# A graph network's convolutions and node sums: weighted sums and totals on ScalarE and VectorE in place of TensorE

## The chip, the core and the metric

One core of a Trainium2 chip runs the whole program. The core has five engines that work from queues of their own: PE (TensorE, matmuls), DVE (VectorE), ACT (ScalarE), POOL (GpSimd) and SP (SyncE, which here only issues DMAs). They meet through semaphores. The metric is device time in microseconds (us) of one execution, lower is better; the time before is the median of three.

## What is computed

The input is a graph: 50,000 nodes with 128 features (`x`) and 25,000 edges sorted by their destination. Two parts follow each other: a sorting convolution with two layers, and a gated recurrent part with five steps. Only the first part is touched by the change:

```
h = relu(layernorm(x))
for layer in 0, 1:
    # up to 4 messages of each node, missing ones filled with blank_p, sorted per feature
    srt = sort(filled, axis=1)                       # (node, 4, 128)
    out = einsum('nmd,m->nd', srt, cw) + cb          # weighted sum of the 4 sorted rows
    u = a * h + out
    mu, var = mean and variance of u over all 50000 nodes, per feature
    h = h + (u - mu) / sqrt(var + 1e-5) * g + be
x = x + h
# then: x + GRU(relu(layernorm(x))), 5 message passing steps
```

All of it is in 32-bit floats.

## The kernel before, in words

The program runs in stages. Stage 1 makes the layer-normed rows `h0_tab` and counts the edges. Then comes one block for each layer: `convolve`, `statistics`, and `apply0` or `apply1`. The recurrent part (all lines from 1400 on) follows.

**`convolve`** handles the edges as 28 groups (NC) of 128 partitions times 7 edges (JC), 896 numbers in each partition. POOL gathers the source rows (L721, seven indirect DMAs a group, into a ring `M` of four) and later scatters the results into `o_tab` (L729, seven more, from a ring `ob` of three, OR). Its program is gather(0), gather(1), gather(2), then gather(i), scatter(i-3) in turn. DVE sorts a group with eleven instructions (L818 to L845) and leaves the four sorted rows in `V[i % 2][0..3]`; the table operands stand in PSUM (`S1`, `L2`, `H2`), so each of these instructions reads at most one operand from SBUF. ACT fills the PSUM operands with the blank row (L750, L776, L777), copies the row before a group (`halo`, L762), and, in `rows(i)` (L784), turns the finished PSUM sum into `ob`. PE forms that sum: eight matmuls per group (L860), each a sorted row times a diagonal matrix `cwi[m]` of the weight. Each f32 matmul stands as two records in the trace. ACT runs `rows(i-1)` after it has prepared group i. SP meanwhile writes the blank rows of the next layer's table.

**`statistics`** reads all rows back in 49 chunks (NCH) of 128 x 1024 numbers: SP loads `hb` and `ob` (512 KB each, rings of four, SR), DVE forms u in `ob` (L907), ACT squares it into `sq` (L938), PE adds u and its square over partitions into two PSUM banks (L948, four matmuls a chunk, a matrix of ones; for the last chunk `ones_last`, which leaves the padding out). SP loads the next chunk when PE has read the old one (`s_pe`). In the same time POOL issues single-column indirect DMAs whose number is fixed: in layer 0 it gathers 196 columns (L661) in all, 120 of them in `statistics` and 76 in `apply0`; in layer 1 it scatters 70 (L658).

**`apply0`** normalises in 49 chunks; DVE has four instructions a chunk (L2233, L2235, L2237, L1050). Before chunk 16 (NCH // 3) DVE runs `slots()`, which waits for all 196 gathered columns; POOL then waits for `slots()` and scatters 126 columns (L658). `apply1` does the same for layer 1 with row statistics, PE transposes and messages (L1174, L1181, L1184) and eight indirect DMAs a chunk on POOL (L1254).

The order on each engine is the order of the code. There is no scheduler.

## Time and profile before

| what | us |
|---|---|
| median of three runs | 5515.18 (5511.57 to 5521.06) |
| span of the one profiled execution | 6564.5 |
| stage 1 | 0 to 337 |
| layer 0: convolve, statistics, apply0 | 337 to 911, to 1292, to 1546 |
| layer 1: convolve, statistics, apply1 | 1546 to 2133, to 2368, to 3121 |
| recurrent part | 3121 to 6564 |

The profile has one execution, taken with the recorder on. Nothing gives this execution's time apart from its span of 6564.5 us. That span is 1049 us longer than the median of the runs without a recorder, so a row of the trace tells of an execution that is a fifth slower than those that are measured. Where the two differ has to be argued, and is, below. Busy shares over the whole span are PE 65%, DVE 59%, ACT 42%, POOL 51%; no engine bounds all stages.

### The profile page before, as it was taken

Reading aid. Unit: us, or ns where it says so; the run is one execution under the profiler, and the core shown is the slowest. Engines: PE = TensorE matmul, PEld = TensorE weight load, DVE = VectorE, ACT = ScalarE, POOL = GpSimd, SP = SyncE. Lnnn points to the kernel's source line nnn. Section 1 sums busy time; section 2 is a strip of 40 time slices with the busy share of each in tenths; the row PEclk is TensorE's granted clock in tenths of the full one; section 3 lists DMA queues with packets and bytes.
Section 4 is the critical chain, followed back from the end, with each engine's and each line's share of the span. In section 5 each row is a group of like instructions: output and inputs, shape, how many; then the busy total and the mean of one; then the engine's idle time right before and its main releaser. Section 6 shows DMA issues by size and latency. Waiting matters only on the chain. (4 is left out here: it accounts for less than half of the span.)

```text
span 6564.5 us, 61506 instructions
## 1 busy us (share of the span) xinstructions
PE 4257.9 (65%) x15022; PEld 2341.7 (36%) x15022; DVE 3845.9 (59%) x7518; ACT 2733.4 (42%) x5325; POOL 3376.4 (51%) x3399
## 2 busy tenths in 40 slices
PE   8944352602344754343577899789889978884586
PEld 5612121300121333232344455455445544442333
DVE  8965530397564255564466676667667756652265
ACT  6822210222222134343476654664465456433432
POOL 8766677046666434544665600640262056556666
PEclk9966676855666877677799999999999999997699
DMA  6722231694111585654476654664465456664444
GB/s 217 256 97 88 80 117 46 238 307 153 40 41 38 195 246 164 179 170 132 140 205 192 213 183 138 201 199 166 150 217 193 138 187 202 214 189 135 123 144 145
DMA packets 628093, 1062.87 MB, mean 162 GB/s; under 512 B 105048, under 2 KB 258158, under 8 KB 627740
## 3 DMA queue, kind: packets, MB, share of 16 engines
q1 hardware_dynamic: 498972, 818.46, 38.6%
q0 software_dynamic: 100544, 163.41, 9.0%
q10 hardware_dynamic: 28224, 77.08, 3.0%
q8 instruction: 126, 2.06, 0.1%
q14 instruction: 227, 1.86, 0.1%
HBM read 599.34 MB, written 464.81 MB: 162 GB/s over the span
## 5 line engine op out<-in xcount | busy, mean ns | idle before, releaser
L1864 POOL DMA_INDIRECT r_G<-msg_tab,srow x784 | 739.6, 943 | 1324.9 <-DMA msg_tab<-r_m 895.0
L860 PE MATMUL l_ps<-cv_V,cv_cwi 128*128 128x448 f32 x896 | 478.3, 702 | 916.7 <-ACT cv_ob L784 457.4
L1254 POOL DMA_INDIRECT x_tab<-a_r,node_pos x392 | 379.6, 968 | 514.7 <-DVE a_r L1211 246.7
L860 PEld LDWEIGHTS l_ps<-cv_V,cv_cwi 128*128 128x128 f32 x896 | 220.4, 253 | 1174.7 <-issue 1161.6
L2113 DVE TENSOR_TENSOR agg<-r_psS,agg 128x128 f32 x980 | 281.7, 287 | 514.7 <-DMA st_o<-o_tab 324.7
L729 POOL DMA_INDIRECT o_tab<-cv_ob,put_idx x392 | 387.7, 989 | 271.9 <-ACT cv_ob L784 147.8
L1945 PE MATMUL r_psR<-r_hin,whh 128*128 128x512 f32 x882 | 463.5, 608 | 27.3 <-ACT r_r L2066 11.4
L1896 PEld LDWEIGHTS r_psM<-wmsg,r_hnew 128*128 128x128 f32 x2744 | 355.8, 195 | 339.5 <-DVE r_hnew L2177 219.1
L1896 PE MATMUL r_psM<-wmsg,r_hnew 128*128 128x128 f32 x2744 | 384.0, 284 | 133.4 <-DVE r_hnew L2177 126.2
L721 POOL DMA_INDIRECT cv_M<-h_tab,gat_src x392 | 373.9, 954 | 119.5 <-issue 119.5
L1181 PE MATMUL l_ps<-a_bmsg,row 128*128 128x512 f32 x196 | 152.5, 871 | 429.3 <-ACT cv_M L1137 271.6
L907 DVE SCALAR_TENSOR_TENSOR st_o<-st_h,ab,st_o 128x1024 f32<-128x1024 f32 x98 | 125.9, 1285 | 507.9 <-DMA st_o<-o_tab 453.2
L784 ACT ACTIVATE cv_ob<-l_ps,cbb 128x896 f32<-128x896 f32 x56 | 56.4, 1007 | 817.5 <-remote 670.4
L948 PE MATMUL l_ps<-st_q,ones 128*128 128x512 f32 x384 | 213.0, 683 | 211.4 <-issue 181.1
L1917 PE MATMUL r_psR<-r_oin,whh 128*128 128x512 f32 x290 | 189.4, 740 | 245.5 <-issue 156.0
L658 POOL DMA_INDIRECT sort_tab<-pair,sort_at x196 | 195.6, 998 | 277.6 <-DVEq L1040 214.1
L1945 PE MATMUL r_psZ<-r_hin,whh 128*128 128x512 f32 x642 | 330.4, 596 | 11.9 <-issue 3.9
L818 DVE COPY_PREDICATED l_ps<-l_ps,cv_M 128x896 f32<-128x896 int32 x56 | 61.5, 1099 | 452.3 <-ACT cv_M L762 399.7
L2129 DVE TENSOR_TENSOR r_m<-r_psM,bmsg 128x512 f32<-128x512 f32 x343 | 235.7, 687 | 150.7 <-remote 80.3
L938 ACT ACTIVATE st_q<-st_o 128x1024 f32<-128x1024 f32 x98 | 103.3, 1056 | 514.5 <-remote 168.6
L1971 PE MATMUL r_psS<-r_sel,r_G 128*128 128x128 f32 x1960 | 293.0, 298 | 28.2 <-DMA r_G<-msg_tab,srow 17.7
L2051 ACT ACTIVATE r_dist<-iota_w,lrank 128x128 f32<-128x128 f32 x980 | 310.0, 390 | 0.0
(292 smaller groups left out, 11307.7 us busy)
## 6 DMA issues: line engine op xcount, KB each, us to landing
r_hin<-ht_tab SPq DMA_DIRECT2D x441, 256.0 KB
msg_tab<-r_m SPq DMA_DIRECT2D x392, 256.0 KB
ht_tab<-r_hnew SPq DMA_DIRECT2D x343, 256.0 KB
o_tab<-o_blank SPq DMA_DIRECT2D x98, 512.0 KB, 6.0
st_h<-h_tab SPq DMA_DIRECT2D x98, 512.0 KB
st_o<-o_tab SPq DMA_DIRECT2D x98, 512.0 KB
r_oin<-ht_tab SPq DMA_DIRECT2D x161, 256.0 KB
i_x<-x_tab SPq DMA_DIRECT2D x49, 528.0 KB
```

What stands on the lines that cost most here:

```text
L721: pool.indirect_dma_start(M[i % CR][:, 1 + q, :], None, h_tab[layer], bass.IndirectOffsetOnAxis(ap=gat_src[:, j:j + 1], axis=0)).then_inc( ...
L729: pool.indirect_dma_start(o_tab[layer], bass.IndirectOffsetOnAxis(ap=put_idx[:, j:j + 1], axis=0), ob[i % OR][:, q, :], None, bounds_check ...
L860: ins = nc.tensor.matmul(psO[:, h, 0:HW], cwi[m][:], V[i % 2][m][:, HW * h:HW * (h + 1)], start=m == 0, stop=m == 3)
L948: ins = nc.tensor.matmul(ps, w[:], t[:, 512 * q:512 * (q + 1)], start=i == 0 and q == 0, stop=i == NCH - 1 and q == 1, skip_group_check=True)
L1254: pool.indirect_dma_start(x2_tab, bass.IndirectOffsetOnAxis(ap=node_pos[:, j:j + 1], axis=0), rb[i % RR][:, t, :], None).then_inc(s_out[i ...
L1864: pool.indirect_dma_start(G[g % GR][:, q, :], None, msg_tab[s % 3] if s else first_tab, bass.IndirectOffsetOnAxis(ap=at, axis=0)).then_inc ...
L1896: ins = nc.tensor.matmul(psM[:, t, :], hnew[k % 2][:, P * t:P * (t + 1)], wmsg[:], start=True, stop=True)
L1945: ins = nc.tensor.matmul(ps, whh[:, g * D:(g + 1) * D], hin[k % 3][:], start=True, stop=not edges)
L1971: nc.tensor.matmul(psS[g % 2][:, q, :], G[g % GR][:, q, :], sel[g % 2][:, q, :], start=True, stop=True).then_inc(s_sel, 1)
L2051: nc.scalar.activation(dist[:, q, :], iota_w[:, 0:SW], ACT.Abs, bias=lrank[:, TQ * i + q:TQ * i + q + 1]).then_inc(s_di, 1)
L2113: nc.vector.tensor_tensor(agg[:, bass.ds(at[q], SW)], psS[g % 2][:, q, :], agg[:, bass.ds(at[q], SW)], ALU.add).then_inc(s_ev, 1)
L2129: nc.vector.tensor_tensor(mb[k % 2][:], psM[:], other, ALU.add).then_inc(s_me, 1)
```

## The change

In `convolve` PE has no work left. ACT multiplies the smallest sorted row by its weight, adds `cb` and writes `ob` (`smallest`, in place of `rows`), and it does so at the end of its turn i, not i+1. DVE adds the other three rows with three dependent `scalar_tensor_tensor` instructions that read `V` and `ob`, both in SBUF. The wait for the ring `ob` (scatter i-3 landed) stands before `smallest`. In `statistics` DVE adds each chunk's u and squares into two running sums of 128 x 1024 in SBUF (they lie in two free `M` buffers), and PE adds these over the partitions once, at the end, with four matmuls. SP reloads `hb` after u is formed and `ob` after u has been added and squared. The four diagonal matrices and `ones_last` go.

```diff
@@ convolve, scalar @@
-                def rows(i):
-                    act.wait_ge(s_mix, i + 1)
+                def smallest(i):
+                    act.wait_ge(s_v0, i + 1)
                     if i >= OR:
                         act.wait_ge(s_sc[i % OR], 16 * JC * (i // OR))
-                    nc.scalar.activation(ob[i % OR][:].rearrange("p j f -> p (j f)").rearrange("p (h n) -> p h n", n=HW),
-                                         psO[:, :, 0:HW], ACT.Identity, bias=cbb[layer][:, 0:1]).then_inc(s_o, 1)
+                    nc.scalar.activation(ob[i % OR][:].rearrange("p j f -> p (j f)"), V[i % 2][0][:], ACT.Identity,
+                                         bias=cbb[layer][:, 0:1], scale=cwb[layer][:, 0:1]).then_inc(s_o0, 1)
...
                     blank_second(i)
-                    if i:
-                        rows(i - 1)
-                rows(NC - 1)
+                    smallest(i)
@@ convolve, vector @@
                     if i >= 2:
-                        dve.wait_ge(s_mix, i - 1)
+                        dve.wait_ge(s_o0, i - 1)
...
                     dve.sem_inc(s_srt, 1)
+                    dve.wait_ge(s_o0, i + 1)
+                    o = ob[i % OR][:]
+                    for k in (3, 1):
+                        st.mark(nc.vector.scalar_tensor_tensor(o, v[k], cwb[layer][:, k:k + 1], o, ALU.mult, ALU.add))
+                        st.wait()
+                    nc.vector.scalar_tensor_tensor(o, v[2], cwb[layer][:, 2:3], o, ALU.mult, ALU.add).then_inc(s_o, 1)
@@ convolve, tensor @@
-                    for h in range(2):
-                        for m in range(4):
-                            ins = nc.tensor.matmul(psO[:, h, 0:HW], cwi[m][:], V[i % 2][m][:, HW * h:HW * (h + 1)],
-                                                   start=m == 0, stop=m == 3)
-                    ins.then_inc(s_mix, 1)
@@ statistics, sync @@
                     if i >= SR:
-                        sp.wait_ge(s_pe, i - SR + 1)
+                        sp.wait_ge(s_u, i - SR + 1)
                         sp.dma_start(hb[i % SR][:], hv[i]).then_inc(s_in[i % SR], 16)
+                        sp.wait_ge(s_au, i - SR + 1)
+                        sp.wait_ge(s_q, i - SR + 1)
@@ statistics, vector @@
+                def squares(i):
+                    m = LASTP if i == NCH - 1 else P
+                    dve.wait_ge(s_q, i + 1)
+                    if i:
+                        dve.wait_ge(s_aq, i)
+                    nc.vector.tensor_tensor(sums[1][0:m, :], sums[1][0:m, :], sq[i % 2][0:m, :], ALU.add).then_inc(s_aq, 1)
...
+                    if i:
+                        squares(i - 1)
+                    dve.wait_ge(s_u, i + 1)
+                    if i:
+                        dve.wait_ge(s_au, i)
+                    nc.vector.tensor_tensor(sums[0][0:m, :], sums[0][0:m, :], ob[k][0:m, :], ALU.add).then_inc(s_au, 1)
+                squares(NCH - 1)
@@ statistics, tensor @@
-                for i in range(NCH):
-                    w = ones_last if i == NCH - 1 else ones
-                    for t, s, ps in ((ob[i % SR], s_u, psU), (sq[i % 2], s_q, psQ)):
-                        pe.wait_ge(s, i + 1)
+                for t, s, ps in ((sums[0], s_au, psU), (sums[1], s_aq, psQ)):
+                    pe.wait_ge(s, NCH)
+                    for q in range(2):
+                        ins = nc.tensor.matmul(ps, ones[:], t[:, 512 * q:512 * (q + 1)], start=q == 0, stop=q == 1,
```

On ACT, in the middle of layer 0's convolution, a turn before reads as follows (`cv0_mixed` is PE's signal, `cv0_put0` a landed scatter):

```order
L776 ACTIVATE l_ps<-blank_p 128x896 [waits cv0_sorted]
L777 ACTIVATE l_ps<-blank_p 128x896
L778 ACTIVATE l_ps<-same 128x7
L784 ACTIVATE cv_ob<-l_ps,cbb 128x896 [waits cv0_put0,cv0_mixed]
L750 ACTIVATE l_ps<-blank_p 128x896 [waits cv0_pairs_done]
```

After the change, on the same engine at the same place (`cv0_smallest` is DVE's signal that the first sorted row is ready):

```order
L770 ACTIVATE l_ps<-blank_p 128x896 [waits cv0_sorted]
L771 ACTIVATE l_ps<-blank_p 128x896
L772 ACTIVATE l_ps<-same 128x7
L778 ACTIVATE cv_ob<-cv_V,cbb,cwb 128x896 [waits cv0_put0,cv0_smallest]
L744 ACTIVATE l_ps<-blank_p 128x896 [waits cv0_pairs_done]
```

The instruction that waits for the landed scatter is now that of the group just prepared, one group earlier than before.

On DVE, a group of the convolution before ends in two sorts and the next begins:

```order
L844 TENSOR_TENSOR cv_V<-cv_A,l_ps 128x896 [waits cv0_dve]
L845 TENSOR_TENSOR cv_V<-cv_A,l_ps 128x896
L818 COPY_PREDICATED l_ps<-l_ps,cv_M 128x896 [waits cv0_dve,cv0_halo,cv0_landed1,cv0_blank1]
```

After the change three instructions stand between them, the first of which waits for ACT (`cv0_rows_begun`):

```order
L832 TENSOR_TENSOR cv_V<-cv_A,l_ps 128x896 [waits cv0_dve]
L833 TENSOR_TENSOR cv_V<-cv_A,l_ps 128x896
L839 SCALAR_TENSOR_TENSOR cv_ob<-cv_V,cwb,cv_ob 128x896 [waits cv0_dve,cv0_rows_begun]
L839 SCALAR_TENSOR_TENSOR cv_ob<-cv_V,cwb,cv_ob 128x896 [waits cv0_dve]
L841 SCALAR_TENSOR_TENSOR cv_ob<-cv_V,cwb,cv_ob 128x896 [waits cv0_dve]
L805 COPY_PREDICATED l_ps<-l_ps,cv_M 128x896 [waits cv0_halo,cv0_landed1,cv0_blank1]
```

In the statistics DVE had one instruction a chunk (L907, 49 times in a row). Now it has three (the sums are called `cv_M`, after the buffers they lie in):

```order
L905 SCALAR_TENSOR_TENSOR st_o<-st_h,ab,st_o 128x1024 [waits st0_in2]
L897 TENSOR_TENSOR cv_M<-cv_M,st_q 128x1024 [waits st0_q_added,st0_q]
L912 TENSOR_TENSOR cv_M<-cv_M,st_o 128x1024 [waits st0_u_added,st0_u]
L905 SCALAR_TENSOR_TENSOR st_o<-st_h,ab,st_o 128x1024 [waits st0_in3]
```

The squares of a chunk are added behind the next chunk's u.

## Rows read from the trace of the kernel before

**Rows 1.** Head of the profile: the span.

```profile
span 6564.5 us, 61506 instructions
```

**Rows 2.** Window, length; PE, PEld, DVE, ACT, POOL busy (count); PEclk; DMA share; GB/s.

```profile
337.00:911.00 574.00, 239.59 (x450) 109.90 (x448) 331.08 (x337) 126.67 (x250) 381.13 (x393) 0.67 0.27 89
911.00:1292.00 381.00, 199.78 (x392) 84.14 (x392) 65.38 (x55) 51.88 (x50) 192.73 (x196) 0.75 0.41 139
1546.00:2133.00 587.00, 239.36 (x448) 110.48 (x448) 319.89 (x315) 127.47 (x252) 384.10 (x396) 0.66 0.15 43
2133.00:2368.00 235.00, 185.45 (x392) 79.71 (x392) 66.23 (x56) 52.04 (x50) 71.13 (x70) 0.87 0.65 220
2368.00:3121.00 753.00, 304.75 (x1335) 214.74 (x1335) 439.91 (x1234) 306.88 (x673) 380.57 (x393) 0.69 0.57 168
3121.00:6564.00 3443.00, 2787.43 (x10330) 1539.32 (x10330) 2084.39 (x3882) 1768.72 (x3361) 1569.61 (x1619) 0.93 0.55 175
```

**Rows 3.** Convolution, layer 0, in time: start, us, engine, line; idle before and its releaser.

```profile
623.71 1.10 DVE L818 COPY_PREDICATED l_ps<-l_ps,cv_M 128x896 f32<-128x896 int32 x1 [22.35 <-ACT cv_M L762]
...
632.31 0.99 POOL L721 DMA_INDIRECT cv_M<-h_tab,gat_src  x1 [0.30 <-issue]
...
635.41 1.10 DVE L818 COPY_PREDICATED l_ps<-l_ps,cv_M 128x896 f32<-128x896 int32 x1 [0.24 <-issue]
...
649.31 8.53 PE L860 MATMUL l_ps<-cv_V,cv_cwi 128*128 128x448 f32 x16 [5.30 <-ACT cv_ob L784]
650.18 0.99 POOL L721 DMA_INDIRECT cv_M<-h_tab,gat_src  x1 [0.31 <-issue]
...
675.63 0.94 POOL L721 DMA_INDIRECT cv_M<-h_tab,gat_src  x1 [0.30 <-issue]
682.65 1.01 ACT L784 ACTIVATE cv_ob<-l_ps,cbb 128x896 f32<-128x896 f32 x1 [30.00 <-remote]
...
684.46 1.01 POOL L729 DMA_INDIRECT o_tab<-cv_ob,put_idx  x1 [7.88 <-ACT cv_ob L784]
```

**Rows 4.** Statistics, layer 0, in time: with POOL issuing, then without.

```profile
1052.02 1.28 DVE L907 SCALAR_TENSOR_TENSOR st_o<-st_h,ab,st_o 128x1024 f32<-128x1024 f32 x1 [20.93 <-DMA st_o<-o_tab]
1052.18 1.94 POOL L661 DMA_INDIRECT look<-node_tab,src_at  x1 [0.30 <-issue]
1074.39 1.29 DVE L907 SCALAR_TENSOR_TENSOR st_o<-st_h,ab,st_o 128x1024 f32<-128x1024 f32 x1 [21.08 <-DMA st_o<-o_tab]
...
1220.61 1.06 ACT L938 ACTIVATE st_q<-st_o 128x1024 f32<-128x1024 f32 x1 [2.38 <-PE l_ps L948]
...
1224.05 1.06 ACT L938 ACTIVATE st_q<-st_o 128x1024 f32<-128x1024 f32 x1 [2.38 <-PE l_ps L948]
```

**Rows 5.** Recurrent part: windows without and with POOL, a group, two rows in time.

```profile
5000.00:5200.00 200.00, 199.28 (x684) 106.78 (x685) 146.09 (x221) 97.26 (x149) 0.00 (x0) 1.00 0.48 161
4100.00:4400.00 300.00, 245.93 (x1099) 145.20 (x1097) 194.79 (x426) 192.95 (x405) 182.19 (x194) 0.97 0.65 202
L1971 PE MATMUL r_psS<-r_sel,r_G 128*128 128x128 f32 x1960 | 293.0, 298 | 28.2 <-DMA r_G<-msg_tab,srow 17.7 <-issue 9.2 <-DVE agg L2113 1.1
3956.02 1.05 PE L1896 MATMUL r_psM<-wmsg,r_hnew 128*128 128x128 f32 x8
3956.91 1.02 PE L1945 MATMUL r_psR<-r_hin,whh 128*128 128x512 f32 x2
```

**Rows 6.** Window 911 to 1165, POOL issuing: count, busy us and mean ns by line.

```profile
L661 POOL DMA_INDIRECT look<-node_tab,src_at x196 | 192.7, 983 | 61.4 <-issue 61.4
L907 DVE SCALAR_TENSOR_TENSOR st_o<-st_h,ab,st_o 128x1024 f32<-128x1024 f32 x20 | 25.8, 1288 | 247.5 <-DMA st_o<-o_tab 201.6 <-issue 45.8
```

**Rows 7.** Line by line: duration in ns, least/median/most.

```profile
L661 POOL DMA_INDIRECT look<-node_tab,src_at x196: 940/944/1962, 911.1 to 1164.0; - x196
L907 DVE SCALAR_TENSOR_TENSOR st_o<-st_h,ab,st_o x98: 1283/1284/1322, 915.8 to 2355.3; 128x1024 f32<-128x1024 f32 x98
L2235 DVE TENSOR_TENSOR l_ps<-l_ps,bn_s x98: 1231/1232/1233, 1295.6 to 3094.7; 128x1024 f32<-128x1024 f32 x98
```

More of the change, by code:

```diff
@@ L127, in build @@
         ones = sb("ones", [P, P])
-        ones_last = sb("ones_last", [P, P])
         later = sb("later", [P, P])
@@ L398, in _ @@
                 st.mark(nc.vector.tensor_scalar(row0[:], ones[:], iota_p[:, 0:1], 0.0, ALU.mult, ALU.is_equal))
-                st.mark(nc.vector.tensor_scalar(ones_last[:], ones[:], iota_p[:, 0:1], float(LASTP),
-                                                ALU.mult, ALU.is_lt))
                 dve.wait_ge(s_src, 16 * 4)
@@ L798, in vector @@
                 tt = nc.vector.tensor_tensor
-                for m in range(4):
-                    nc.vector.tensor_scalar(cwi[m][:], ident[:], cwb[layer][:, m:m + 1], None, ALU.mult
-                                            ).then_inc(s_wt, 1)
                 dve.wait_ge(s_f1, 2)
@@ L847, in group, with statistics @@
                     dve.sem_inc(s_srt, 1)
+                    dve.wait_ge(s_o0, i + 1)
[4 more added lines that the diff above has]
+                    nc.vector.scalar_tensor_tensor(o, v[2], cwb[layer][:, 2:3], o, ALU.mult, ALU.add).then_inc(s_o, 1)
                 for i in range(NC):
                     group(i)
-            def tensor(pe):
-                pe.wait_ge(s_wt, 4)
-                for i in range(NC):
-                    pe.wait_ge(s_srt, i + 1)
-                    if i:
-                        pe.wait_ge(s_o, i)
-                    for h in range(2):
-                        for m in range(4):
-                            ins = nc.tensor.matmul(psO[:, h, 0:HW], cwi[m][:], V[i % 2][m][:, HW * h:HW * (h + 1)],
-                                                   start=m == 0, stop=m == 3)
-                    ins.then_inc(s_mix, 1)
-            return vector, tensor, scalar, gpsimd, sync, filled_up, scattered, low + high + M, V[0] + V[1]
-        def statistics(layer, c, banks, table, idx, cols, j0, j1, scatter):
+            return vector, scalar, gpsimd, sync, filled_up, scattered, low + high + M, V[0] + V[1]
+        def statistics(layer, c, banks, spare, table, idx, cols, j0, j1, scatter):
             n = f"st{layer}_"
@@ L877, in statistics @@
             sq = [sb(f"{n}q{i}", [P, RT * D], F32, c) for i in range(2)]
+            sums = [t[:, 0:RT, :].rearrange("p t f -> p (t f)") for t in spare]
             tot = sb(n + "tot", [P, 2, D], F32, c)
@@ L942, in tensor @@
             def tensor(pe):
[L943 to L950 removed]
+                for t, s, ps in ((sums[0], s_au, psU), (sums[1], s_aq, psQ)):
+                    pe.wait_ge(s, NCH)
+                    for q in range(2):
+                        ins = nc.tensor.matmul(ps, ones[:], t[:, 512 * q:512 * (q + 1)], start=q == 0, stop=q == 1,
+                                               skip_group_check=True)
                     ins.then_inc(s_pe, 1)
@@ L1329, in _ @@
             def _(pe):
-                cv_tensor(pe)
                 st_tensor(pe)
```

38 lines of the change are left out of this document (18 added, 20 removed).

## The prediction

> **What bounds the kernel now.** I read the head first, then the busy time by stage, then single turns of each stage in order of time.
>
> The head says 6564.5 us [rows 1], the median of the runs 5515.18. The 1049 us between them must be placed before anything is costed, since the stages that the change touches could hold them. By stage, PE is busy for 239.59 of 574 us in the first convolution and POOL for 381.13; neither is full there [rows 2]. One turn shows why. PE starts its 16 records of a group at 649.31 and the last of them ends 8.53 us later, at 657.8. ACT needs only this sum and a scatter that was issued 50 us before, but starts at 682.65, with an idle time of 30.00 us that is put down to nobody. POOL issues DMAs without a gap until 676.6; then it waits 7.88 us for ACT [rows 3]. So PE's signal reaches ACT 25 us after its last record, 6 us after POOL fell silent. The statistics repeat it: while POOL issues, chunks are 22.4 us apart (1052.02 to 1074.39), though DVE works 1.28 us on each, and without POOL they are 3.44 apart (1220.61 to 1224.05) [rows 4]. I read this as a late signal of PE beside POOL's DMAs.
>
> Is it there without the recorder? The recurrent part answers in part. A window of 200 us in which POOL issues nothing has 684 PE records at 199.28 us busy, at a granted clock of 1.00 (the 2.4 GHz level): 3.42 records in a us [rows 5]. The part has 10,330 records [rows 2], of which 1,960 are the small ones of L1971 [rows 5]; a small record takes 0.89 / 8 = 0.11 us (3956.02 to 3956.91). Without a pause PE needs some 8,370 / 3.42 + 1,960 x 0.11 = 2,660 us. So of 5515 us at most about 2,855 are left for all before it, where the trace has 3121: over 260 us of the excess lie in stages 1 to 3, and more if PE pauses at all. Freed of the late signals those stages come to about 2,485 (below), and the recurrent part to 5515 - 2485 = 3,030, between that floor and its 3443. I take it that the late signals come with the recorder and cost the measured runs little.
>
> So the stages as they run without it: stage 1 337. **Convolution**: a POOL turn is seven gathers and seven scatters, 632.31 to 650.18, 17.87 us; 28 of them 500. DVE's group takes 635.41 - 623.71 = 11.7 [rows 3]. POOL bounds it. **Statistics**: 49 x 3.44 = 169, PE bounds it; 182 with 13 for its first loads and its end. **Apply of layer 0**: 254, from 1292 to 1546. DVE bounds it: four instructions of 1.23 to 1.29 (L2235 and L907's kind [rows 7]), 5.0 a chunk, 245, and so 9 for `slots()`. **Apply of layer 1**: POOL bounds it with eight DMAs a chunk at 0.97 + 0.30, 10.2 us, 500; 520 with 20 around it. The 13, 20 and 10 for the second convolution's start are allowances. Sum: 337 + 500 + 182 + 254 + 510 + 182 + 520 = 2,485.
>
> **The change part by part.** *PE leaves the convolution.* PE and L784 were hidden under POOL's 17.87, so nothing is gained in the measured time. ACT's instruction is as long as before (1.01) and hidden.
>
> *Three more DVE instructions per group.* L907, the same operation on 1024 numbers, takes 1.284 us [rows 7]; on 896 it is 1.12, with a dependence 1.15. DVE's group becomes 11.7 + 3.4 = 15.1, still under 17.87. The last group's chain gets shorter (3.4 in place of 8.5 and 1.0), behind four scatters of 9 us: zero.
>
> *The moved wait.* Now ACT's turn i waits for scatter i-3, which POOL issues in its own turn i. Queued behind it are ACT's preparation of group i+1, and on DVE the three additions and group i+1. The landing comes once a turn, 17.87 apart whatever a landing takes; between two of them ACT needs 1.0 and DVE 15.1, some 16.2 with the signals. So it fits, with 1.7 us to spare, and POOL asks for this group's rows only three turns later: zero. It would cost if a turn of POOL fell below about 16.2.
>
> *POOL is held by the new instructions.* At 1052.18 a DMA issue starts 0.16 us behind the start of L907 and takes 1.94 us, where 0.94 is usual; it ends 0.82 us after L907's end [rows 4, 7]. L907 reads two operands from SBUF. The sorts read at most one from SBUF, and the issues that run beside them take 0.94 to 0.99 [rows 3]. In the window 911 to 1165, 196 issues take 192.7 us, 7.7 above 196 x 0.944, beside 20 L907: 0.38 us for each [rows 6, 7]. All three new instructions read two operands from SBUF. Bounds: zero, if a POOL issue always slips between; and 1.0 for each (1.94 - 0.94), 3.0 a group, 168 us over 56 groups. They stand back to back, 1.15 apart, and POOL's next issue comes 1.25 behind a released one, so I count two of three at 0.38: 0.77 a group, **43 us** for both layers, since POOL is the bound there.
>
> The Trainium skill, page "SBUF — State Buffer", section "Who interferes with whom", states the rule behind this: a DVE instruction with two SBUF inputs and a GpSimd instruction that reads SBUF exclude each other, and the one issued second waits until the other is finished. On POOL's side the trace agrees (1962 ns against 944 [rows 7]). On DVE's side it does not: L907 never took over 1322 ns [rows 7]; the rule's sum is rival 4.
>
> *Statistics.* PE's 3.44 us a chunk goes; DVE now has 1.28 + 2 x 1.23 (L2235, two operands on 1024 numbers [rows 7]) = 3.75 at most, and 3.63 if each overlaps the next by 0.04 as the sorts do (eleven of 1.10 in 11.7). Against 3.44 that is 9 to 15 us a layer; I take 15, as the adds wait on each other's signals. It is the bound in layer 1: **+15**. Its POOL columns, 70 x 1.3 = 91 us, stay covered.
>
> *Layer 0 behind it* is tied between two engines. Counted from the end of the convolution, DVE reaches `slots()` at 182 + 16 x 5.0 = 262, POOL has its 196 columns at 196 x 1.25 = 245; DVE ends at 182 + 254 = 436 and POOL at 262 + 9 + 126 x 1.29 = 433 (a scatter takes some 0.04 more than a gather, 17.87 being 7 of each). After: DVE reaches `slots()` at 277. POOL, held by three such instructions a chunk (two of three at 0.38, times 49 = 38), is done at 283, so DVE waits 6 and ends at 457: **+21**. Bounds: +8, where neither happens in full, and +54, where POOL gets two issues into a chunk in place of three.
>
> `ones_last` and the four diagonals go, five instructions on 128 numbers, and four matmuls after a long pause of PE come at the end: zero.
>
> **Sum**: 43 + 15 + 21 = 79. 5515 + 79 = **5594 us**. Against the profiled execution the sum has another sign: the late signals go with PE's work. Convolutions 574 and 587 become some 525 and 535, layer 0 behind it 635 becomes 457, statistics of layer 1 235 becomes 197, the rest stays: a span near 6564 - 101 - 178 - 38 = 6,250.
>
> **The rivals.** *1. The late signals are real in the measured runs (faster).* Place: ACT's wait before L784, SP's wait for PE before a reload. For: the rows themselves, and that my argument against rests on a floor. Against: the 260 us above. If the recurrent part ran at its floor, 2,855 would be left before it, 370 above the undelayed sum; the touched stages hold 400 of the trace's 634, so 230 would go, and 79 come: 5515 - 150 = 5,365. With half of it, 5,480. It decides from about a third of the delay (80 us) on.
>
> *2. POOL is not held, or DVE's chunk is under 3.44.* For: singles often slipped through. Then the statistics' 9 to 15 us a layer are left, 5,533 to 5,545, and with the loads as the bound nothing, 5515. The loads (2 x 512 KB in 3.44 us, 305 GB/s) may bound the chunk either way.
>
> *3. POOL issues faster without the recorder.* The 0.30 us between two issues [rows 3] is idle time. Without it a turn is 14 x 0.96 = 13.5, and DVE's 15.1, 16.2 with ACT's part, becomes the bound: 1.6 to 2.7 x 56 = 90 to 150, with 15 a layer 120 to 180: 5,635 to 5,695, and 5,650 taken. Against: the sum of 2,485 would fall by some 300 and the recurrent part would have to be nearly all of its 3443.
>
> *4. DVE is held by POOL as well* (the page's rule). Each new instruction would wait up to 0.94: 15.1 + 2.8 = 17.9 a group beside POOL's own delays, and half of that in each chunk of the statistics, 1.4 x 98 = 137: above 5,700. Against: 1322 ns at most.
>
> **How the numbers follow.** What a measurement of this kernel can tell from no change is about 0.2%, 11 us: faster is below 5504, slower above 5526. My forecast (5,560 to 5,640) 0.48. Rival 2: 0.20, a half within 11 us. Rival 3: 0.15. Rival 4 and the upper bounds: 0.05. Rival 1: 0.12, a sixth of it within 11 us. So faster 0.10, same 0.12, slower 0.78. The predicted time is the likeliest case's, 5594. For 8 in 10 I go from 5505 to 5690: below lies most of rival 1 (0.10), above a tenth of the rest.
>
> **What would show it.** In the trace after: ACT's new instruction starts within 2 us of the last landed scatter and never stands 25 us idle; the three additions 1.12 to 1.15 each; POOL's turn 17.9 to 19, with single issues of 1.3 to 2.0 us only beside them; DVE's group near 15 with waits for POOL. Chunks of the statistics 3.6 to 3.8 apart from first to last; the 126 scatters begin 280 to 290 us behind the convolution. Span near 6,250 while the measured time rises. The forecast is wrong if the measured time falls with the span (rival 1), if POOL's turns stay at 17.87 (rival 2), or if DVE is never idle in the convolution (rivals 3 and 4).

## The result, and the profile after

| | us | against before |
|---|---|---|
| before, median of four runs beside it | 5513.38 | |
| after, median of four runs | 5546.19 (5545.44 to 5554.37) | 1.0062, 95% interval 1.0050 to 1.0073 |
| predicted | 5594 | +79, measured +33 |

The kernel became slower, inside the range, by less than half of the forecast. A second set of runs, on another chip, gives 1.0056 (1.0042 to 1.0070) for the same pair. Differences in us below are the ratio, less one, times the time before. Ratios are made of the undisturbed runs alone, so they leave out one run of e9 (7442 us) and, on the one chip where before spreads from 6319 to 6558 us, its nine runs above 6,450.

The span of the profile after is 5543.7 us at a run of 5545.44: the profile now shows what is measured. Before, it did not. Two things stand on record on that. In all four sets of runs below every run has a recorded span, 1.7 to 2.0 us below its time; so these measured runs were recorded too, and the recorder does not explain the excess. And one of the four chips of these sets takes 6319 to 6558 us for the kernel before, with the late signals in the trace of e12 (e10 to e12 below). The profile of before with its 6564.5 us most likely comes from such a chip; which chip it was is not on record. So a second profile of before (5505.2 us of a run of 5506.97) stands here as the yardstick. Head and busy time by window, of the kernel after, with the columns of [rows 2]:

```profile
span 5543.7 us, 58821 instructions
```

```profile
335.00:841.00 506.00, 1.82 (x3) 0.34 (x1) 428.27 (x419) 131.61 (x250) 386.27 (x394) 0.50 0.31 101
841.00:1027.00 186.00, 5.16 (x8) 2.06 (x8) 176.37 (x157) 53.94 (x52) 153.08 (x109) 0.52 0.84 283
1318.00:1821.00 503.00, 0.00 (x0) 0.00 (x0) 417.28 (x397) 131.71 (x250) 383.87 (x392) 0.50 0.17 48
1821.00:2007.00 186.00, 5.12 (x8) 2.03 (x8) 174.48 (x161) 54.03 (x52) 166.80 (x64) 0.52 0.90 291
2533.00:5543.00 3010.00, 2691.66 (x10301) 1513.69 (x10299) 2077.64 (x3882) 1776.81 (x3349) 1569.49 (x1620) 0.96 0.63 200
```

The same windows (convolution, statistics, of each layer, and the recurrent part) of the kernel before, recorded again:

```profile
335.00:839.00 504.00, 238.71 (x451) 109.36 (x449) 331.27 (x337) 129.66 (x250) 381.00 (x393) 0.69 0.31 102
839.00:1020.00 181.00, 170.47 (x392) 75.19 (x392) 66.90 (x58) 53.85 (x52) 139.84 (x121) 0.97 0.82 291
1294.00:1793.00 499.00, 237.64 (x448) 109.38 (x448) 319.20 (x311) 129.57 (x250) 379.90 (x392) 0.69 0.17 48
1793.00:1976.00 183.00, 170.60 (x392) 75.19 (x392) 67.18 (x59) 53.22 (x51) 81.72 (x71) 0.97 0.86 286
2503.00:5505.00 3002.00, 2700.04 (x10292) 1519.69 (x10292) 2077.33 (x3882) 1776.35 (x3347) 1569.12 (x1619) 0.96 0.63 200
```

The convolutions took 504 and 499 us and take 506 and 503: +6 in both, though DVE has 97 us more work in each (428.27 against 331.27). The statistics took 181 and 183 and take 186 each. The rest is a wait. This is the instruction with which DVE begins the slots, before (recorded again) and after:

```profile
1114.89 0.26 DVE L1027 CAST pf<-look 128x196 f32<-128x196 int32 x1 [14.59 <-DMA look<-node_tab,src_at]
```

```profile
1139.22 0.26 DVE L1029 CAST pf<-look 128x196 f32<-128x196 int32 x1 [32.01 <-DMA look<-node_tab,src_at]
```

It starts 276 us behind the end of the convolution before (1114.9 - 838.6) and 298 after (1139.2 - 840.7). In both DVE waits for POOL's columns; now for longer: **+22 us**. From there on the chains are alike, down to the end of the last scatter 170 us later (1285.6 and 1309.5).

So the stages give 6 + 22 + 3 (layer 1's statistics) = 31 of the +33 (layer 0's statistics lie within the 22). The recurrent part shows 3010 against 3002, but the 13 profiles of before, after and the variants on such chips show 3002 to 3012 there, without relation to the edits.

Why POOL is late stands in the statistics. Group of POOL's column issues in the window 843 to 1010, before (again) and after: count, busy us and mean ns.

```profile
L661 POOL DMA_INDIRECT look<-node_tab,src_at x110 | 129.5, 1177 | 33.5 <-issue 33.5
```

```profile
L658 POOL DMA_INDIRECT look<-node_tab,src_at x97 | 139.2, 1435 | 29.6 <-issue 29.6
```

An issue that is not held takes 0.944 us (the median of all 196). Before, POOL lost 110 x (1.177 - 0.944) = 26 us in the window, after 97 x (1.435 - 0.944) = 48: 22 us more. And here is a chunk after, in time:

```profile
900.88 1.27 DVE L905 SCALAR_TENSOR_TENSOR st_o<-st_h,ab,st_o 128x1024 f32<-128x1024 f32 x1
902.07 1.26 DVE L897 TENSOR_TENSOR cv_M<-cv_M,st_q 128x1024 f32<-128x1024 f32 x1
902.08 0.94 POOL L658 DMA_INDIRECT look<-node_tab,src_at  x1 [0.30 <-issue]
...
903.26 1.21 DVE L912 TENSOR_TENSOR cv_M<-cv_M,st_o 128x1024 f32<-128x1024 f32 x1
903.33 1.96 POOL L658 DMA_INDIRECT look<-node_tab,src_at  x1 [0.30 <-issue]
904.39 1.27 DVE L905 SCALAR_TENSOR_TENSOR st_o<-st_h,ab,st_o 128x1024 f32<-128x1024 f32 x1
...
905.59 0.95 POOL L658 DMA_INDIRECT look<-node_tab,src_at  x1 [0.30 <-issue]
```

DVE repeats every 3.51 us. POOL gets exactly two issues into that: one that starts 0.01 us behind an addition and is not held (0.94), and one that starts 0.07 us behind the next and is held until that one's end at 904.47 (1.96, ends 0.82 later). 0.94 + 0.30 + 1.96 + 0.30 = 3.50: the two rhythms are locked.

### The profile page after: what moved, and what is told of

Read it like the earlier page. It is cut to its first block and busy times, and to the rows that moved or that the text cites. A ratio compares the mean times of both kernels' runs of the same rounds, so it can differ in the third digit from the quotient of the medians.

```text
span 5543.7 us, 58821 instructions
## 1 busy us (share of the span) xinstructions
PE 3289.9 (59%) x13358; PEld 1926.2 (35%) x13358; DVE 4236.5 (76%) x7877; ACT 2754.7 (50%) x5325; POOL 3530.2 (64%) x3399
## 3 DMA queue, kind: packets, MB, share of 16 engines
q8 instruction: 113, 1.85, 0.1%
## 5 line engine op out<-in xcount | busy, mean ns | idle before, releaser
L778 ACT ACTIVATE cv_ob<-cv_V,cbb,cwb 128x896 f32<-128x896 f32 x56 | 63.5, 1133 | 626.1 <-DMA o_tab<-cv_ob,put_idx 487.5
L1896 PE MATMUL r_psM<-wmsg,r_hnew 128*128 128x128 f32 x2744 | 363.9, 276 | 3.9 <-DVE r_hnew L2177 3.9
L655 POOL DMA_INDIRECT sort_tab<-pair,sort_at x196 | 297.4, 1517 | 69.2 <-issue 61.6
L1971 PEld LDWEIGHTS r_psS<-r_sel,r_G 128*128 128x128 f32 x1960 | 260.7, 207 | 207.2 <-DMA r_G<-msg_tab,srow 203.5
L1907 PE MATMUL r_psHN<-r_hin,whh 128*128 128x512 f32 x560 | 290.0, 600 | 7.0 <-DMA r_hin<-ht_tab 7.0
L287 POOL TENSOR_SCALAR hot_hi<-iota_w,hif 128x392 bf16<-128x392 f32 x196 | 268.7, 1386 | 30.9 <-DVE occ L314 24.2
L2085 ACT ACTIVATE r_r<-r_psR,brz 128x512 f32<-128x512 f32 x245 | 168.3, 687 | 227.3 <-PE r_psR L1951 227.3
L658 POOL DMA_INDIRECT look<-node_tab,src_at x196 | 235.7, 1203 | 61.4 <-issue 61.4
L2156 DVE TENSOR_TENSOR r_t<-r_t,r_psI 128x512 f32<-128x512 f32 x196 | 134.9, 688 | 182.7 <-PE r_psI L2023 182.7
```

The lines of the kernel that those rows point to most:

```text
L655: ins = pool.indirect_dma_start(table, at, cols[:, j, :], None, bounds_check=EPAD - 1, oob_is_err=False)
L1896: ins = nc.tensor.matmul(psM[:, t, :], hnew[k % 2][:, P * t:P * (t + 1)], wmsg[:], start=True, stop=True)
L1907: nc.tensor.matmul(psHN[k % 2][:], whh[:, 2 * D:3 * D], hin[k % 3][:], start=True, stop=True).then_inc(s_hn, 1)
L1971: nc.tensor.matmul(psS[g % 2][:, q, :], G[g % GR][:, q, :], sel[g % 2][:, q, :], start=True, stop=True).then_inc(s_sel, 1)
```

## Experiments

Four sets of runs, each with the kernel before beside it. The first two and the last fell on chips where before takes 5514 to 5523 us.

**e0: the kernel before, recorded again.** No edit.

> The kernel before, unchanged, recorded once more. The kernel after was recorded at a span of 5543.7 us, which is its measured time; the kernel before had 6564.5 against 5515. Theory A: that recorded execution of before stood alone; a second one has a span of about 5,515 us, PE's signal reaches ACT within 2 us, the convolutions take about 500 and 510 us, the statistics 182 each, the applies 254 and 520, the recurrent part about 3,030 (the sums of the prediction). Rival (my prediction's reading): the late signals come with the recorder wherever PE works beside POOL's DMAs; then the span is about 6,560 again with 574 and 587 us for the convolutions. The measured time is the same in both, 5,515 within 0.1%.

Measured: 5520.16 against 5523.04, span 5505.2. PE's signal is on time: L784 starts 0.03 us behind the last matmul of its group (619.13 + 8.48 = 627.61).

```profile
619.13 8.48 PE L860 MATMUL l_ps<-cv_V,cv_cwi 128*128 128x448 f32 x16 [9.03 <-DVEq L847]
```

```profile
627.64 1.01 ACT L784 ACTIVATE cv_ob<-l_ps,cbb 128x896 f32<-128x896 f32 x1 [6.68 <-PE l_ps L860]
```

So the recorder does not delay PE's signals, and the stages are those of theory A (504, 181, 499, 183, 3002). At this point I took the profile of before for a single odd execution; e10's set showed a chip on which each execution is so slow.

**e1 and e2: one part of the change alone.** e1 takes `convolve` of the kernel after and `statistics` of the kernel before; e2 the other way round.

```diff
@@ e1: all of convolve @@
-                    act.wait_ge(s_mix, i + 1)
+                    act.wait_ge(s_v0, i + 1)
...
-                cv_tensor(pe)
@@ e2: all of statistics @@
-                        sp.wait_ge(s_pe, i - SR + 1)
+                        sp.wait_ge(s_u, i - SR + 1)
```

> Only the convolutions are changed: ScalarE and VectorE form the weighted sums; the sums over all nodes stay on PE as before. Theory A (the kernel after shows POOL's turn at 17.9 us in nearly all groups, since DVE and POOL fall into a rhythm in which the three additions meet gaps or few issues): 0 to +9 us against before. Prediction's term: +43 us for both layers. Rival B (the whole +33 comes from here): +33 us.

> Only the statistics are changed: VectorE adds the chunks into two running sums in SBUF; the convolutions keep PE. Theory A (POOL's columns are held up beside the additions with two SBUF operands, 105 instead of about 145 of them issued during the 182 us of layer 0, so that VectorE waits some 30 us before the slots): +25 to +33 us. Prediction's terms: +15 +21 less the convolution's share, about +30, with chunks 3.75 us apart. Rival B: 0 to +5 us.

Measured: e1 5526.85 against 5523.04, ratio 1.0012 (1.0003 to 1.0021), +7; e2 5544.14, ratio 1.0042 (1.0029 to 1.0056), +23, a little under theory A's +25. They add up to +30. (The expectation of e2 calls the prediction's share "about +30"; it put +15 on layer 1 and +21 on layer 0, most of it from the statistics.) The prediction's +43 for the convolutions falls. In e2 POOL issues as in the kernel after (97 issues, mean 1431 ns in the same window), with PE still in the convolutions: the hold comes from the statistics' own additions.

**e3: the two running sums in PSUM.** The 98 additions then read one operand from SBUF and one from PSUM.

```diff
-            sums = [t[:, 0:RT, :].rearrange("p t f -> p (t f)") for t in spare]
+            flat = [t[:, 0:RT, :].rearrange("p t f -> p (t f)") for t in spare]
+            sums = [banks[2][:], banks[3][:]]
...
+                for t, ps, s in ((flat[0], sums[0], s_au), (flat[1], sums[1], s_aq)):
+                    dve.wait_ge(s, NCH)
+                    nc.vector.tensor_copy(t, ps).then_inc(s_flat, 1)
```

> The kernel after, with the two running sums of the statistics in PSUM (and copied to SBUF once, 2.5 us a layer), so that the 98 additions read one operand from SBUF and one from PSUM. Theory A: POOL is no longer held beside them; its columns in layer 0 go from 1.75 to about 1.33 us apart, VectorE's wait of 32 us before the slots falls to a few, and of the +33 us of the change some 25 go: +5 to +12 against before. Rival B (the hold on POOL does not matter, the additions' own time on VectorE or the loads do): +33 to +38, as the kernel after or worse by the copies.

Measured: 5552.51, ratio 1.0061 (1.0047 to 1.0074), +34: nothing gained. Theory A in its simple form fell. The timeline shows what it had missed:

```profile
900.15 1.23 DVE L914 TENSOR_TENSOR l_ps<-l_ps,st_o 128x1024 f32<-128x1024 f32 x1
900.23 0.95 POOL L658 DMA_INDIRECT look<-node_tab,src_at  x1 [0.30 <-issue]
901.28 1.28 DVE L907 SCALAR_TENSOR_TENSOR st_o<-st_h,ab,st_o 128x1024 f32<-128x1024 f32 x1
...
901.48 1.91 POOL L658 DMA_INDIRECT look<-node_tab,src_at  x1 [0.30 <-issue]
...
903.69 0.95 POOL L658 DMA_INDIRECT look<-node_tab,src_at  x1 [0.30 <-issue]
904.74 1.28 DVE L907 SCALAR_TENSOR_TENSOR st_o<-st_h,ab,st_o 128x1024 f32<-128x1024 f32 x1
...
904.94 1.90 POOL L658 DMA_INDIRECT look<-node_tab,src_at  x1 [0.30 <-issue]
```

The additions in PSUM hold nothing. But L907, which forms u and which the kernel before has too, still reads two operands from SBUF, and it now catches one issue in every chunk: held until L907's end at 902.56, released, one issue free, and the one after that starts 0.20 us into the next L907. Still two issues a chunk.

**e6 and e7: u from PSUM as well.** ScalarE copies each chunk of `o` to PSUM first. e6 is e3 with that; e7 is the kernel before with only that.

```diff
+                def copy(i):
+                    act.wait_ge(s_in[i % SR], 32 * (i // SR + 1))
+                    if i >= 2:
+                        act.wait_ge(s_u, i - 1)
+                    nc.scalar.activation(px[i % 2], ob[i % SR][:], ACT.Copy).then_inc(s_cp, 1)
...
+                    dve.wait_ge(s_cp, i + 1)
-                    nc.vector.scalar_tensor_tensor(ob[k][:], hb[k][:], ab[layer][:, 0:1], ob[k][:],
+                    nc.vector.scalar_tensor_tensor(ob[k][:], hb[k][:], ab[layer][:, 0:1], px[i % 2],
```

> As e3_stats_psum (the kernel after, running sums of the statistics in PSUM), and in addition ScalarE copies each chunk of `o` to PSUM first, so that u = a h + o reads one operand from SBUF and one from PSUM too: no VectorE instruction of the statistics reads two operands from SBUF. e3 left POOL at one held issue a chunk (two issues in 3.44 us, 1.72 us apart), all of them beside the forming of u. Theory C (a single instruction with two SBUF operands a chunk is enough to hold one issue in each chunk, since VectorE's regular 3.44 us and POOL's held pair lock to each other): now no issue is held, all 0.944, 1.25 us apart, 196 columns in 245 us; VectorE reaches the slots first, about 265 us behind the convolution in place of 298 (after) and 276 (before); of the +33 us of the change all go: -5 to +6 against before. Rival D (the hold has nothing to do with where the operands lie): as e3, +33.

> The kernel before, with only this: ScalarE copies each chunk of `o` to PSUM in the statistics and VectorE forms u from SBUF and PSUM. Theory C: before, too, POOL's columns bound layer 0 (issues 1.48 us apart in the statistics, 51 of 109 held); freed they come 1.25 apart, the slots begin some 12 us earlier, where VectorE reaches them: -10 to -13 us, ratio near 0.998. Rival (the prediction's reading: VectorE bounds layer 0 before, POOL is done 17 us ahead of it): 0.

Measured: e6 5520.59 against 5513.72, ratio 1.0011 (1.0002 to 1.0020), +6; e7 5503.57, ratio 0.9980 (0.9971 to 0.9989), -11. Both as theory C said. The same window 843 to 1010 in e6: 131 issues where the kernel after has 97, and a mean of an issue that is never held.

```profile
L658 POOL DMA_INDIRECT look<-node_tab,src_at x131 | 124.0, 946 | 44.3 <-issue 44.3
```

DVE now goes from its last row straight into the slots (1109.41, 267 us behind the convolution's end at 842.2), without a wait:

```profile
1108.27 1.22 DVE L1069 TENSOR_TENSOR cv_low<-l_ps,ap_h 128x1024 f32<-128x1024 f32 x1
1109.41 0.25 DVE L1046 CAST pf<-look 128x196 f32<-128x196 int32 x1
```

So 28 of e3's 34 us were this hold. And e7 shows that POOL, not DVE, bounded layer 0 before the change as well.

**e8 and e9: is it the offset that spares the convolutions?** In the kernel after the additions of a group and POOL's issues stand like this:

```profile
710.36 0.95 POOL L715 DMA_INDIRECT cv_M<-h_tab,gat_src  x1 [0.30 <-issue]
...
710.47 2.34 DVE L839 SCALAR_TENSOR_TENSOR cv_ob<-cv_V,cwb,cv_ob 128x896 f32<-128x896 f32 x2
...
711.61 0.94 POOL L715 DMA_INDIRECT cv_M<-h_tab,gat_src  x1 [0.30 <-issue]
...
712.85 1.15 DVE L841 SCALAR_TENSOR_TENSOR cv_ob<-cv_V,cwb,cv_ob 128x896 f32<-128x896 f32 x1
712.86 0.94 POOL L715 DMA_INDIRECT cv_M<-h_tab,gat_src  x1 [0.30 <-issue]
```

The additions start at 710.47, 711.66 (the first two share a row, which ends at 712.81, and one takes 1.15) and 712.85, the issues at 710.36, 711.61 and 712.86: each issue is ahead of an addition or level with it, and none is held. It is not so from the start: of the first eleven turns of POOL in layer 0 five take 18.8 us, each with one issue held for 1.85 to 1.89; from then on they take 17.87 to 17.89, but for one of 18.17. e8 puts one more instruction of 0.95 us ahead of the additions; e9 does the same and lets the weighted sum grow in PSUM.

```diff
@@ e8 and e9 @@
                     st.mark(tt(v[2], A[:], L2, ALU.max))
+                    st.mark(tt(late_by[:], A[:, 0:6], L2[:, 0:6], ALU.min))
@@ e9 @@
-                    o = ob[i % OR][:]
+                    o = psW[:, 0:JC * D].rearrange("p (j f) -> p j f", f=D)
...
+                    if i >= OR:
+                        dve.wait_ge(s_sc[i % OR], 16 * JC * (i // OR))
-                    nc.vector.scalar_tensor_tensor(o, v[2], cwb[layer][:, 2:3], o, ALU.mult, ALU.add).then_inc(s_o, 1)
+                    nc.vector.scalar_tensor_tensor(ob[i % OR][:], v[2], cwb[layer][:, 2:3], o, ALU.mult, ALU.add).then_inc(s_o, 1)
```

> The kernel after, with one more VectorE instruction in each group of the convolutions, ahead of the three additions (a minimum of 128x768, about 0.95 us, into a buffer that nothing reads). VectorE keeps slack: 16.1 of 17.87 us. Theory E (POOL is hardly held in the convolutions of the kernel after because its issues start 0.12 us before, 0.07 before and 0.01 before the three additions in nearly every group, and this offset repeats itself, since VectorE's group is clocked by POOL's own gather): moved by 0.95 us, an issue starts 0.2 us into the first addition in each turn and is held for about 0.8 us, 56 times: +45 over the kernel after, +65 to +85 against before, and POOL's turn near 18.7. Rival F (the holds average 0.1 us a group whatever the offset, or VectorE's slack is all that matters): nothing over the kernel after, +30 to +40 against before.

> As e8_shift, with the same instruction ahead of the additions, but the weighted sum grows in PSUM: ScalarE writes the first term there, each of VectorE's three additions reads one operand from SBUF and one from PSUM, and the last writes `ob`. Theory E: no issue can be held, whatever the offset: POOL's turn 17.87, -2 to -8 us against the kernel after, +25 to +31 against before. Rival G (what e8 adds is VectorE's or ScalarE's own time, not the hold): as e8.

Measured: e8 5573.41 against 5513.72, ratio 1.0107 (1.0092 to 1.0122), +59, some 25 over the kernel after; e9 5537.17, ratio 1.0043 (1.0030 to 1.0056), +24. In e8 the second of these issues starts 0.29 us into an addition, and is held until 0.82 us behind that one's end (701.85 + 1.15 = 703.00, 703.82):

```profile
700.89 0.94 POOL L716 DMA_INDIRECT cv_M<-h_tab,gat_src  x1 [0.30 <-issue]
...
701.85 2.34 DVE L841 SCALAR_TENSOR_TENSOR cv_ob<-cv_V,cwb,cv_ob 128x896 f32<-128x896 f32 x2
...
702.14 1.68 POOL L716 DMA_INDIRECT cv_M<-h_tab,gat_src  x1 [0.30 <-issue]
704.12 0.95 POOL L716 DMA_INDIRECT cv_M<-h_tab,gat_src  x1 [0.30 <-issue]
```

All issues of both convolutions, gathers and scatters, of the kernel after, of e8 and of e9:

```profile
L723 POOL DMA_INDIRECT o_tab<-cv_ob,put_idx x392 | 392.3, 1001 | 119.4 <-issue 118.4 <-DVE cv_ob L841 0.9
L715 POOL DMA_INDIRECT cv_M<-h_tab,gat_src x392 | 378.4, 965 | 119.4 <-issue 119.4
```

```profile
L716 POOL DMA_INDIRECT cv_M<-h_tab,gat_src x392 | 401.7, 1025 | 119.4 <-issue 118.8 <-DVE cv_ob L843 0.6
L724 POOL DMA_INDIRECT o_tab<-cv_ob,put_idx x392 | 398.2, 1016 | 119.4 <-issue 116.9 <-DVE cv_ob L843 2.4
```

```profile
L724 POOL DMA_INDIRECT o_tab<-cv_ob,put_idx x392 | 387.8, 989 | 119.4 <-issue 118.8 <-DVE cv_ob L845 0.6
L716 POOL DMA_INDIRECT cv_M<-h_tab,gat_src x392 | 373.9, 954 | 119.4 <-issue 118.5 <-DVE cv_ob L845 0.6 <-ACT cv_M L757 0.3
```

Their sums are 770.7, 799.9 and 761.7 us (before, again: 387.8 + 373.7 = 761.5). What the holds cost in the convolutions is thus 9 us after and 38 in e8, and the time follows: +29 by these sums, +25 measured. 12 of 784 issues take over 1.1 us after, 53 in e8, none before. My +45 for e8 was too high, since 41 more holds came, at 0.7 each, not 56 at 0.8. In e9 the holds are gone although the instruction ahead is there, and so is their cost. Both came out a little below their ranges: e8 +59 for +65 to +85, e9 +24 for +25 to +31.

**e10: a longer chunk.** e3 with one more instruction of 128x256 in each chunk.

```diff
+                    nc.vector.tensor_tensor(longer[:], ob[k][:, 0:256], sums[0][:, 0:256], ALU.min).then_inc(s_lg, 1)
+                    dve.wait_ge(s_lg, i + 1)
                     nc.vector.tensor_tensor(sums[0][0:m, :], sums[0][0:m, :], ob[k][0:m, :], ALU.add).then_inc(s_au, 1)
```

> As e3_stats_psum (running sums in PSUM, only the forming of u reads two operands from SBUF), with one more VectorE instruction of 128x256 in each chunk of the statistics (one operand from SBUF, one from PSUM, into a buffer that nothing reads), so that VectorE's chunk grows from 3.44 to about 3.9 us. Theory C (the two rhythms lock: after a held issue POOL's next ones start 1.13 and 2.38 us behind the end of the instruction that held it, and the next such instruction starts 2.16 us behind it in e3, so that each second issue is caught; with 3.9 us it starts 2.6 behind it, the second one slips by and only the third is caught): three issues a chunk in place of two, 1.30 us apart in place of 1.72, though VectorE has more to do; VectorE is then the last at the slots, about 285 us behind the convolution (e3: 294), layer 0 ends some 5 earlier and layer 1's statistics end 21 later: +15 over e3, about +50 against before. Rival H (one of two issues is held whatever the rhythm, or the hold goes with the share of time in which such an instruction runs, 1.28 of 3.44): two issues a chunk or fewer, the slots near 310 to 320 us behind the convolution: +40 or more over e3, about +75 against before.

The first set with it fell on a chip where the kernel before takes 6425.87 us (see e11, e12); the second on one with 5517.21.

> The kernel of e10_longer_chunk, again, because its first runs fell on a chip on which the kernel before takes 6,426 us and the chunks of the statistics are 4.9 us, so that the two rhythms could not be read. On a chip with before near 5,515, theory C: chunks of 3.9 us, three issues a chunk, 1.30 us apart, about +15 over e3, +50 against before. Rival H: two issues a chunk or fewer, +75 against before.

Measured there: 5563.69, ratio 1.0088 (1.0075 to 1.0102), +49 against the +50 of theory C. A chunk of POOL:

```profile
930.21 0.94 POOL L658 DMA_INDIRECT look<-node_tab,src_at  x1 [0.30 <-issue]
931.45 0.94 POOL L658 DMA_INDIRECT look<-node_tab,src_at  x1 [0.30 <-issue]
932.70 1.11 POOL L658 DMA_INDIRECT look<-node_tab,src_at  x1 [0.30 <-issue]
934.12 0.95 POOL L658 DMA_INDIRECT look<-node_tab,src_at  x1 [0.30 <-issue]
```

Three issues in 3.91 us. DVE's chunk grew by 13% (3.44 to 3.89), and the same 196 columns were done 258 us behind the convolution where e3 needed 291 (1099.5 - 841.6, 1133.6 - 842.0). The hold does not go with the share of time in which a two-operand instruction runs; the rhythm sets it. The longer chunk costs more than that gains, so e10 as a whole is slower than e3.

**e11 and e12: no addition on two SBUF operands.** e11 is e6 with e9's sum in PSUM (without the extra instruction). e12 has that convolution and e7's statistics, whose sums stay with PE.

> Both parts of the change with all of its additions freed from a second SBUF operand: the statistics as in e6_stats_free, the convolution's weighted sum grown in PSUM as in e9_shift_psum but without the extra instruction. Theory: e6 stood at +6; the convolutions end 4 to 9 us earlier than the kernel after's, as in e9: -4 to +2 against before, so within the noise of it: taking work off TensorE is worth nothing in itself. Rival: the lower granted clock of TensorE ahead of layer 1's apply costs something that no PSUM operand cures: +5 or more.

> A version meant to beat both: the convolution's weighted sum on ScalarE and VectorE in PSUM (as e9 without the extra instruction), the sums over all nodes on TensorE as in the kernel before, and ScalarE copies `o` to PSUM ahead of u (as e7_before_free). e7 stood at -10; the convolutions of e9 ended 3 us earlier than those of before: -8 to -15 us against before, ratio 0.9973 to 0.9985. Rival: nothing beyond e7 (-10), since POOL bounds the convolutions in both and only its holds can differ.

Measured on the chip with 6425.87 (6319 to 6558) for before: e10 6384.76, ratio 1.0034 (1.0003 to 1.0065); e11 6304.51, ratio 0.9911 (0.9875 to 0.9946); e12 6542.75, ratio 1.0284 (1.0247 to 1.0321). All 43 runs of that set are slow, whatever the kernel, and it is the only set on that chip. The ratios are firm in one point alone: six of e11's seven runs (6278 to 6322) are faster than the fastest of before. The runs of e10 (6362 to 6413) and e12 (6526 to 6551) lie within the spread of before, so that e12 loses there is not shown. The trace of e12 there has the late signals of [rows 4], and e12 keeps PE in the statistics. Beside POOL's unbroken issues, ACT waits 16 us for PE (it needs PE to have read the old squares), whose last matmul before it ends at 1048.81, and DVE 21 for its next chunk, which SP loads on the same signal (at 1064.44):

```profile
1064.51 1.06 ACT L939 ACTIVATE st_q<-st_o 128x1024 f32<-128x1024 f32 x1 [16.23 <-remote]
```

```profile
1070.80 1.28 DVE L899 SCALAR_TENSOR_TENSOR st_o<-st_h,ab,l_ps 128x1024 f32<-128x1024 f32 x1 [21.15 <-ACT l_ps L930]
```

That freeing POOL costs e12 there, by putting more issues beside PE's signals, is an argument; no run there separates it.

> The kernel of e11_all_free, again, for the same reason. On a chip with before near 5,515: -4 to +2 us against before (e6 stood at +6, the convolutions of e9 ended 5 and 4 us earlier than those of the kernel after); rival +5 or more. On a chip like the last one: 0.991 again.

> The kernel of e12_free_pe_sums, again, for the same reason. On a chip with before near 5,515: -8 to -15 us, ratio 0.9973 to 0.9985; rival: no more than e7 (-10). On a chip like the last one: 1.028 again, since the sums over the nodes stay with PE there and POOL, no longer held, issues without a gap beside them.

Measured on the chip with 5517.21: e11 5508.13, ratio 0.9988 (0.9979 to 0.9997), -7; e12 **5500.57**, ratio **0.9974 (0.9964 to 0.9983)**, **-14**. e11 gained more than its -4 to +2; e12 is in its range. e12 beats both kernels on such a chip. Against e7 (-11, 0.9971 to 0.9989, in another set) its gain is not clear of the noise, so that taking PE out of the convolutions gains anything is not shown: the rival of e12's expectation stands. The version that takes PE out of both stages (e11, 5508.13) is 8 us slower than the one that takes it out of the convolutions alone (e12), though neither has an instruction of the change that reads two operands from SBUF.

**e13: the kernel after, beside these.** No edit.

> The kernel after, unchanged, beside the three that follow on the same chip. On a chip like those of the first two sets (before near 5,515): ratio 1.005 to 1.007, +28 to +38 us. On a chip like that of the last set (before 6,426, with PE's signals late as in the profile of before): theory K (there the change takes PE's late signals out of the path): the time falls against before, ratio 0.985 to 0.995, since e10 with the same parts stood at 0.9934 there.

Measured: 5545.05 against 5517.21, ratio 1.0056 (1.0042 to 1.0070), +31. The 0.9934 that its expectation gives for e10 is a misreading: e10 stood at 1.0034 there. The kernel after itself was not run on the slow chip, so theory K, and whether the change would gain there, stays open.

## Why the prediction was right and wrong

*Head and late signals.* That the late signals cost the measured runs little was right, and so was the floor that led there: freed stages of 500, 182, 510 and 182 came out as 504, 181, 499 and 183, the recurrent part's 3,030 as 3002. Layer 0's apply and the next start, 254 and 10, came out as 274 (1020 to 1294), which has POOL's lateness in it (below). The reason given, that they "come with the recorder", was wrong: e0 was recorded at 5505.2 with its signals on time, and on one of the four chips of these sets before takes 6,426. The span forecast of 6,250 therefore fell (5543.7). That the profile's 6564.5 and the 5515 of the runs were two chips, the likeliest reading now, is a possibility that the prediction did not list. The argument from the floor did not rest on that reason.

*The convolutions, +43: the step that failed.* It took an average hold (0.38 us for each two-operand instruction, from 20 instances), counted two of three additions in each group, and multiplied. No such average holds: DVE's group starts on POOL's gather (the 41.5 us that L805 waits in layer 0 end with it), so the offset between additions and issues nearly repeats itself, turn after turn, and it settled where the issues start ahead of the additions or level with them. Measured +6 in the traces and +7 in e1; POOL's holds come to 9 us in all. With another offset (e8) they are 38, near the 43. Between the bounds of 0 and 168 the value has to come from the offset; the trace of before, which has no such additions in its convolutions, does not give it.

*The statistics' chunk, +15 in layer 1: too high.* It was 3.75 against 3.44. The three instructions sum to 3.74, but each starts 0.07 to 0.08 us before the one ahead ends, not 0.04, so a chunk takes 3.49 us on average in layer 0 and 3.45 in layer 1; and PE's 3.44 is 3.40 in the second profile of before. Measured +3 (186 against 183). Its 70 columns "stay covered", but barely, since the hold on them was put at nothing: 91 us were forecast, and POOL needs 194 (1822.1 to 2016.6; before 102). Its first issue of layer 1's apply follows at 2017.07, 0.45 us later, when DVE releases it.

*Layer 0 behind the convolution, +21: right in size (+22), for two errors that cancel.* The prediction had POOL 17 us ahead of DVE before the change and let it lose 38. In fact POOL was already behind (L1027 waits 14.59 us before the change), as its columns were costed at 1.25 apart although L907 cost 110 of them 26 us; and it lost 22 more. POOL's hold went from 26 to 48 us, an increase of 0.45 a chunk in place of the 0.77 assumed. That the two errors cancel is luck. "POOL gets two issues into a chunk in place of three", named as the upper bound of +54, is what happened, but from a start of 2.2 issues a chunk (110 in 167 us, at 3.40 a chunk), not three.

*PE's leaving, the moved wait, the constants, at zero:* they hold. ACT's new instruction starts on the landed scatter, DVE still has idle time in each group (L805 waits 41.5 us in 28 groups of layer 0), and layer 1's apply begins and lasts as before (527 us).

*The rivals.* Rival 2 (POOL not held) is what the convolutions show, though by their offset. Rival 4 fell: the additions take 1150 to 1216 ns in all 168 cases. Rival 3 fell: POOL's turns stay at 17.87 us and more, with the 0.30 between issues, in executions whose span is the measured time. Rival 1's premise, late signals in measured runs, is real on the other kind of chip; what it would give the change there was not run.

## What to carry to other kernels

Where an engine is held only if two rhythms meet, do not multiply an average: ask which engine clocks the other. Where the held engine clocked the other, as in these convolutions, the offset settled and repeated, for good (9 us) or ill (38 us, e8); where it did not, as in the statistics, what counted was how many of its periods fit into the other's, held ones included. A free operand place in PSUM removed the question on the usual chips, at the price of one ScalarE copy. And when a profile's span and the measured time differ by a fifth, have the same kernel recorded again before a reason is built on it.

## What the runs showed of the hardware

- POOL's indirect DMA issue (0.944 us) is held when a DVE instruction with two SBUF operands has started well before it and still runs. In the trace of the kernel after every gather or scatter of the convolutions and every column of layer 0 that starts 0.10 us or more into such an instruction ends 0.81 us or more behind that instruction's end (904.47 to 905.28 after, 902.56 to 903.38 in e3). Of 73 that start 0.05 us or less into one (902.08, 712.86) 72 are not held. Between 0.06 and 0.09 both occur: 48 of 51 columns are held (903.33), none of 6 issues of the convolutions. In e6, with one operand in PSUM, the longest of 131 issues took 0.995 us.
- On the slow chip that is not all. In e11 and e12 there 40 and 66 of the 784 issues of the convolutions take over 1.1 us, up to 1.69, and no DVE instruction with two SBUF operands runs beside any of them. In the traces of after and before (again), on the usual chips, each of the 62 and 33 such issues among gathers, scatters and columns of layer 0 has one beside it. What slows them on the slow chip stays open.
- The scatters of layer 1 beside the statistics are held through more than one addition: 3.16 us each, one a chunk. Why these and not the gathers of layer 0 was not tried. They run 10 us past the end of the statistics (2007 to 2016.6) and cost nothing there, by a margin of 0.45 us.

```profile
1897.17 3.16 POOL L655 DMA_INDIRECT sort_tab<-pair,sort_at  x1 [0.31 <-issue]
1900.63 3.17 POOL L655 DMA_INDIRECT sort_tab<-pair,sort_at  x1 [0.30 <-issue]
```

- One of the four chips runs this program at 6319 to 6558 us in place of 5505 to 5529, with signals from PE that come 15 to 25 us late while POOL issues DMAs (1048.81 to 1064.51 in e12, 657.8 to 682.65 in the first profile of before). What sets such a chip apart stays open, and whether the order of two versions can turn round with it: e12 is 0.9974 on one kind and 1.0284 on the other, but there within the spread of before.
- TensorE's granted clock was 0.50 (the 1.2 GHz level) in the convolutions without PE's work, 0.69 with it, 0.52 in the statistics of the kernel after and 0.97 (near the 2.4 GHz level) in those of the kernel before. Layer 1's apply took 527 us where PE had worked before it (before) and 526 where it had not (after).
